# A fused attention and feed-forward layer on one core: shift rows issued ahead of the gap stores and key strips, and the early double steps closed up by two places

## What is computed

```python
q = (x @ wq).reshape(B, S, 16, 16); k = (x @ wk).reshape(B, S, 4, 16); v = (x @ wv).reshape(B, S, 4, 16)
q = q * cos + rotate_half(q) * sin;  k = k * cos + rotate_half(k) * sin
scores = einsum('bqkgd,bskd->bkgqs', q.reshape(B, S, 4, 4, 16), k) / sqrt(16)
out = einsum('bkgqs,bskd->bqkgd', softmax(scores), v).reshape(B, S, 256) @ wo
x = layernorm(x + out)
Wg, Wu, Wd = (gate_w - 128) * gate_scale[:, None], ...          # int32 weights, inner width 1024
x = layernorm(x + (silu(x @ Wg.T) * (x @ Wu.T)) @ Wd.T)
```

## Time and profile before

| | |
|---|---|
| median of 3 runs | 899.76 us |
| lowest, highest | 895.79, 901.49 us |
| profiled execution | 895.75 us, of which the span from first to last instruction is 893.9 us |
| PE busy | 873.9 us, 98% of the span |
| DVE, ACT, POOL busy | 740.8, 711.2, 272.4 us |
| mean granted TensorE clock | 0.995 |

### The profile page before, as it was taken

How to read it: one execution, slowest core, us unless ns; L and a number is a source line. 1 busy time by engine, 2 the same in 40 slices (tenths; PEclk the granted TensorE clock), 3 DMA queues, 4 the chain that set the end, 5 groups by cost and what they waited for, 6 DMA issues and landing times.

```text
span 893.9 us, 16212 instructions
## 1 busy us (share of the span) xinstructions
PE 873.9 (98%) x5658; PEld 457.1 (51%) x5658; DVE 740.8 (83%) x1653; ACT 711.2 (80%) x928; POOL 272.4 (30%) x236
## 2 busy tenths in 40 slices
PE   9999999999999999999999999999999999999996
PEld 3334334444444444434444444444436888888885
DVE  5679889999999999999999999999955455665545
ACT  2468889999999999999999999999985466555564
POOL 6564540045334010001001000210104665665555
PEclk9999999999999999999999999999999999999998
DMA  8973543423342122122223313121112010110001
GB/s 302 259 199 105 145 117 90 95 76 86 105 114 58 45 78 71 52 70 67 52 59 82 74 45 78 45 70 31 35 55 57 25 48 24 48 48 25 25 24 48
DMA packets 53458, 69.98 MB, mean 78 GB/s; under 512 B 17344, under 2 KB 26560, under 8 KB 53376
## 3 DMA queue, kind: packets, MB, share of 16 engines
q1 hardware_dynamic: 50280, 65.53, 26.8%
q0 software_dynamic: 864, 3.15, 1.2%
q10 hardware_dynamic: 2232, 0.25, 0.2%
HBM read 46.74 MB, written 16.25 MB: 70 GB/s over the span
## 4 chain that ended last, share of the span: by engine, by line
PE 86%; DVE 5%; SPq 3%; ACT 2%; DMA 2%; issue 2%; POOL 0%; POOLq 0%; DVEq 0%; ACTq 0%
PE pv_bank L1434 26%; PE ring_bank L1344 24%; PE pair_bank L1493 13%; PE pair_bank L1562 12%; PE pv_bank L1588 3%; PE ring_bank L1588 3%; PE ring_bank L1444 2%; DVE block_max L907 2%; PE pair_bank L1382 1%; ACT probs L1246 1%; DMA ident<-identity 1%; SPq L351 1%; PE ring_bank L1459 1%; DVE above L903 1%; SPq L491 1%
## 5 line engine op out<-in xcount | busy, mean ns | idle before, releaser
L1246 ACT ACTIVATE probs<-pair_bank 128x1024 f32<-128x1024 f32 x512 | 495.9, 1023 | 46.6 <-PE pair_bank L1493 46.5
L907 DVE TENSOR_REDUCE block_max<-ring_bank 128x1 f32<-128x384 f32 x854 | 486.3, 609 | 16.5 <-PE ring_bank L1344 6.4
L1344 PE MATMUL ring_bank<-k_max,q_sb 48*128 48x512 f32 x1122 | 309.0, 441 | 3.0 <-DMA k_max<-k_parts 1.4
L1344 PEld LDWEIGHTS ring_bank<-k_max,q_sb 48*128 48x128 f32 x1122 | 148.4, 184 | 268.8 <-DVE block_max L907 118.2
L1434 PE MATMUL pv_bank<-probs,v_all 128*17 128x512 f32 x2048 | 270.5, 600 | 0.6 <-ACT probs L1246 0.5
L1493 PE MATMUL pair_bank<-q_sb,k_sb 50*128 50x512 f32 x1024 | 219.8, 426 | 5.5 <-DMA q_sb<-shift 2.2
L1099 DVE SCALAR_TENSOR_TENSOR hid<-pair_bank,up_s,silu 128x512 f32<-128x512 f32 x63 | 47.1, 748 | 84.6 <-ACT silu L1304 84.6
L1493 PEld LDWEIGHTS pair_bank<-q_sb,k_sb 50*128 50x128 f32 x1024 | 97.8, 185 | 32.5 <-ACT probs L1246 6.4
L727 POOL TENSOR_TENSOR attn<-attn,inv_rows 128x1024 f32<-128x1024 f32 x7 | 16.7, 2384 | 301.4 <-DMA inv_rows<-inv_d 301.4
L812 POOL TENSOR_TENSOR hid_l<-hid,hid_h 128x512 fp32r<-128x512 f32 x63 | 81.7, 1297 | 86.1 <-ACT hid_h L1283 85.4
L1191 ACT ACTIVATE above<-ring_bank 128x512 f32<-128x512 f32 x138 | 81.9, 597 | 15.9 <-PE ring_bank L1344 10.1
(11 more groups left out here) (149 smaller groups left out, 863.0 us busy)
## 6 DMA issues: line engine op xcount, KB each, us to landing
k_max<-k_parts SPq DMA_DIRECT2D x96, 96.0 KB, 3.1
q_sb<-q_parts SPq DMA_DIRECT2D x64, 128.0 KB, 2.9
k_sb<-k_parts SPq DMA_DIRECT2D x96, 64.0 KB, 2.4
attn<-xT SPq DMA_DIRECT2D x8, 512.0 KB, 7.2
q_parts<-high SPq DMA_DIRECT2D x16, 256.0 KB, 3.5
q_parts<-low SPq DMA_DIRECT2D x16, 256.0 KB, 3.9
q_sb<-q_parts SPq DMA_DIRECT2D x64, 64.0 KB, 3.0
attn<-pv_sb SPq DMA_DIRECT2D x128, 32.0 KB
```

The lines of the kernel that those rows point to most:

```text
L907: dve.reduce_max(block_max[half % 2][:, col:col + 1], bank[:, 0:width], axis=AX.X).then_inc(ring_used, 1)
L1246: act.activation(probs[t % 2][:, 2 * pr:2 * pr + 2, :], pair_bank[pr][:], ACT.Exp, scale=D ** -0.5).then_inc(probs_ready, 1)
L1344: pe.matmul(bank[:, 0:last - first], q_sb[k][rows, i, qt * P:(qt + 1) * P], k_max[k // QH][rows, kind * CH + first:kind * CH + last], star ...
```

## The change

SP's order in pair 0: `load_shift` now stands ahead of `store_gap(k)` and `swap_strips(k+1)`; `swap_strips(1)` keeps its place. `load_scales` goes from half 1 of pair 0 to half 1 of pair 1. The twelve double steps are spread over 22 places in place of 24: they stand on 24, 25, 27, 29, 31, 33, 35, 36, 38, 40, 42, 44, that is (4,0), (4,1), (4,3), (4,5), (5,1), (5,3), (5,5), (6,0), (6,2), (6,4), (7,0), (7,2).

```diff
+LAST_STEP = 46
@@
         for i in range(2 * LEAD):
-            early[divmod(FIRST_STEP + i // 2 * (BLOCKS * HOOKS - FIRST_STEP) // LEAD, HOOKS)].extend(step(i))
+            early[divmod(FIRST_STEP + i // 2 * (LAST_STEP - FIRST_STEP) // LEAD, HOOKS)].extend(step(i))
@@
                         store_pv(p - 1 if k == 0 else p, (k - 1) % HALVES)
-                    if first and k > 0:
-                        store_gap(k)
-                        if k < B - 1:
-                            swap_strips(k + 1)
@@
                         load_shift(p + 1, 0)
                     if first and k == 0:
                         prologue_over()
-                        swap_strips(1)
+                    if first and k > 0:
+                        store_gap(k)
                     if first and k < B - 1:
+                        swap_strips(k + 1)
                         bring_half(k + 1)
                         store_k(k + 1)
-                    if first and k == 1:
+                    if p == 1 and k == 1:
                         load_scales()
```

## The result

The changed kernel took 901.32 us in the median of 20 runs (897.56 to 905.27), against 899.60 us for 20 runs of the kernel before. The ratio is **1.0026, 95% interval 1.0014 to 1.0038**: 2.3 us slower, where 2.2 us faster were forecast. Nine microseconds would be 1%, so this is a small loss, but it has the wrong sign.

The account below looks back on a forecast made before the run. PE was taken as the bound, busy 873.9 of 893.9 us, so queue edits pay only where PE stands still. The terms -2.36 (SP's order) and +0.2 (start) gave -2.2, from 899.76 to 897.6 us, range 892 to 901.5.

Parts of the forecast that it names:

- The two stalls: PE idle 1.90 us ahead of half 2 and 2.16 us ahead of half 3 in pair 0, together costing 4.27 us.
- the order is not what delays PE: Rival: ACT's writes or DMA queues delay the shift rows; stalls stay or shrink little, 899.3 us; chance 0.15.
- with the longer `load_q`: Variant for half 3 in pair 0: load_q takes 2.91 us, 0.6 us of stall stays, gain 1.3 us.
- Part 1: Shift rows ahead in SP's queue, pair 0: two old stalls go, one new comes; gain 2.36 us.
- The second stall goes too: Ahead of half 3: PE may start at 123.76 and wants it at 124.18, 0.4 us to spare.
- From the strips' end to the low key store 4.86: SP's queue, pair 0: strips' landing and POOL's work take 4.86 us and move with the strips.
- A new stall of 1.9 us: Ahead of half 4: SP's backlog lets PE start at 144.96, where it wants 143.05.
- I take nothing for it: Clock at the loop's start, half 0: a smoother start might return 1.7 to 3.4 us; counted as zero.
- Part 3: Closer double steps in the prologue: first scores 0.4 to 1.7 us later, DVE gives back up to 1.5; 0.2 us slower.
- the first shift rows come late: Rival, prologue: place (6,2) slips by d, first scores by d - 0.3; outweighs 2.36 from d = 2.7; 902.3 us; chance 0.10.
- A cover of 0.3 us: Prologue: the last first shift row lands at 63.7, PE's first scores start at 64.15; slack put at 0.3 us.
- Part 2: load_scales moved: frees 1.98 us of SP in pair 0's half 1; costs nothing in pair 1, at most 1.98 us.

Follow-up runs that it names:

- experiment 1: Only the closer double steps (22 places), SP's order as in the kernel before: 900.6 us, ratio 1.0008 to the kernel before.
- experiment 2: Changed kernel with the double steps on the old 24 places, so only SP's order and the scales move: 899.99 us, ratio 1.0000 to the kernel before.
- experiment 4: Changed kernel with SP's first shift rows issued ahead of block 5's second query store: 897.72 us, ratio 0.9984 to the kernel before.
- experiment 12: The kernel of experiment 2 run again, unchanged, for a second trace: 897.02 us.
- experiment 3: The kernel of experiment 2 with the gap stores moved behind the strips: 894.79 us, ratio 0.9946 to the kernel before.
- experiment 5: The changed kernel itself again, on a second chip: 901.2 us, ratio 1.0004 to the kernel before.
- experiment 11: The kernel before run again, unchanged, for a second trace: 900.47 us, an execution near its median.
- experiment 10: Experiment 3 (double steps on 24 places) with the first shift rows ahead of block 5's second query store: 894.39 us, ratio 0.9956 to the kernel before.
- experiments 13 to 15: Experiment 3's SP order, one chip, ratios to kernel before: 22 places with early first shift rows 0.9938; 24 places with them 0.9953; 22 places without 0.9952.
- experiment 6: Experiment 3 with the closer double steps on 22 places: 897.26 us, ratio 0.9967 to the kernel before.
- experiment 8: Experiment 3 with load_scales back in half 1 of pair 0: 894.74 us, ratio 0.9944 to the kernel before.

## Why the prediction was wrong

The forecast was 2.2 us faster: 2.4 from SP's order, less 0.2 for the start. Measured were 2.3 us slower, and 0.4 for the same kernel on a second chip. The experiments give nothing for SP's order. For the start the traces give about 1.6 us of loss, and experiment 1 gives 0.7, with an interval from 0.5 gained to 2.0 lost.

**What held.** The two stalls are SP's order, not ACT's writes and not the DMA queues, so the rival "the order is not what delays PE" falls. The stall ahead of half 2 goes in all five traces of the changed order (the changed kernel twice, experiments 2, 4 and 12), and a new one comes ahead of half 4 for the reason given; experiment 3 cuts it to 0.67 us by SP's order alone. In the profiled execution halves 1 to 4 gained 1.42 us of the 2.36, close to the 1.3 us that the prediction gives "with the longer `load_q`". That is luck: `load_q` was not the cause, and the four other traces of this order gained next to nothing there.

**First failed step: the 2.36 us of Part 1.** Forecast were 77.4 us for halves 1 to 4. Experiment 4 has 79.6 without any half clock, and experiments 2, 5 and 12 have 79.5 to 79.8 once the excess of half 4 over 18.87 us is taken out, against 79.75 in the profile of before. The 2.2 us that are missing are three terms:

- "The second stall goes too": 0.62 to 0.65 us of it stay in all five traces. "From the strips' end to the low key store 4.86" was 6.24 in the profile and 5.7 to 6.3 in the others, since POOL got its strips late: in the profile one of their four DMAs took 3.3 us to land and the others 2.0 to 2.1.
- "A new stall of 1.9 us" is 2.46 to 2.50 us in four traces, and 1.18 only in the profiled one. In the four the strips of the second pass took 3.2 to 3.5 us to issue, in the profile 2.45.
- A half between stalls was taken at its steady 18.87 us. Half 2 lost another 0.70 to 1.07, in all five traces together with a DVE shift instruction that ended just after POOL's. This term was put at nothing without a word; moving the strips back also moved POOL's work under DVE's.

**The clock: a term left out, but not the cause of this loss.** "I take nothing for it" was said of the start alone, and stalls were priced at their length. They are the start of half-clock stretches too: 10.2, 6.8 and 3.4 us behind the new stall in experiments 2, 5 and 12, and 10.2 us behind the second stall of the kernel before in experiment 11. It is tempting to say that the change turned a gain into a clock loss. The runs don't bear it out: the mean granted clock of the changed kernel is 0.9911 and, on the second chip, 0.9918, that of the kernel before there 0.9885. SP's order alone gains nothing at equal clock either (experiment 2). What the clock does show is why an order that leaves no stall over 0.7 us gains 4.9 us, more than the 3.4 us of its halves 1 to 4, and why one forced stall costs 7.5. Within a kernel a run's span falls as its mean clock rises: the correlation is -0.8 to -0.95 in each kernel up to experiment 10, and -0.1 to -0.9 on the chip of experiments 13 to 15, with 6 to 11 runs each. On the chip of experiments 1 to 4 the kernel before has 894.3 to 895.2 us of span in runs at 0.993 and 898.6 to 900.1 at 0.986. The prediction saw the profile at 0.995 lie 4.0 us under the median and shifted it by 4.0 without asking for their cause.

**Second failed step: "I take 0.2 us slower" of Part 3.** The start lost 2.71 us, not 0.4 to 1.7: 1.66 by PE itself, and 1.05 by shift rows that came late. Bank waits come to about 2.57 us (at (4,1), (5,3), (6,0) and (6,4)) against 1.7 in the kernel before; the rest fits the projections that now stand alone between steps (the key and value projection of a block took 2.02 us in two parts and 1.87 in one). Half 0 gave back 22.29 - 21.20 = 1.09 us, within the 1.5 of Part 3, and the profile lost 1.6 in all; experiment 1 measured 0.7, experiment 6 against 3 1.9. The 1.6 lie outside Part 3's own ends, of which the upper, 1.2, left out that the whole 1.7 could be lost. That is the rival "the first shift rows come late". Its deciding point was d = 2.7, and d was 2.84. Its price came from the rows of the prologue; what it lacked was a chance above 0.10. Its 902.3 us lie near the 901.32 measured, but that is in part luck: it has the 2.36 us of Part 1 in it, which did not come, and a second half-clock stretch at the start, which the profile does not have. "A cover of 0.3 us" in the earlier trace rows was the warning: any delay beyond it goes to the end in full.

**Part 2** is tested only on the repaired order: there the scales cost nothing in pair 0 (experiment 8). In pair 1 they may not be free, as Part 2 had it: 11 of the 13 traces with the scales moved have a wait of 0.10 to 0.49 us ahead of the first scores of half 6, the four without the move have none. That is small, and no experiment was made on it.

**The sum.** Parts alone: 1.0008 and 1.0000. Together 1.0026 and 1.0004, which agree with each other and with the sum only at their edges. The changed kernel is 0.4 to 2.3 us slower: a start that got 1.6 us longer, and a gain that was laid out from one trace and isn't there in the others.

**What stays open.** Why a stall of about 2.5 us is followed by 0, 3, 7 or 10 us at half clock in kernels that are alike there; no run here separates the cases. (The Trainium skill, "TensorE: Matmul & The Clock Gate", section "What's actually happening", says that the gate's watch runs free and doesn't start with the kernel, so that one kernel meets it in another phase each time. The unequal stretches behind equal stalls agree with that, and show no more of it.) And why one strip DMA lands late: in all five traces of the changed order it coincides with a transfer of 0.02 MB by an instruction queue, which in both traces of before falls on `load_scales` or `load_q` instead (the longer `load_q` of Part 1). In the four traces with a new stall of 2.5 us a second such transfer falls into the slow strips of the second pass, 1.3 to 1.8 us after their start; in the profiled execution it comes 1.5 us after their end. These are coincidences in time; no experiment moved one. In the changed kernel, DMA activity from 109 to 110 us, its instruction queue (packets, MB, share) and the strip DMA under way (KB, us to landing):

```profile
q8 instruction: 1, 0.02, 7.1%
...
k_by_sin<-k_turn SPq DMA_DIRECT2D x1, 64.0 KB, 3.3
```

## What to carry to other kernels

Before pricing a stall by its length, look whether the profiled execution is a usual one: if its clock and time are the best of its runs, take another trace near the median, and look for half-clock stretches behind the same stall. Before calling the clock the cause, compare the mean granted clocks of the two kernels over all runs, and their times at the same clock. Where stalls of one cause come in a row, an edit that leaves one long one may gain nothing; here what paid was to leave none over 0.7 us. A reordering shifts the other engines' work too: look what it now runs beside. In a queue that waits for another engine's answer, put the request first (the strips) and fill the wait with what nobody needs (the gap stores); and before closing work up ahead of a chain with 0.3 us of cover, move that chain's own issue forward.

## What the runs showed of the hardware

TensorE's granted clock fell from 2.4 to 1.2 GHz within 2 us of the end of stalls of 1.95 to 2.52 us in a PE that was busy before (experiments 1, 2, 5, 11, 12), for 3.4 to 10.2 us. It stayed up behind stalls of 2.46 us (experiment 4), 2.51 (ahead of half 2 in experiment 11), and 1.90 and 2.16 us. A stall 3.85 us longer than before cost 7.5 us with the half clock behind it, and about 4 in the runs without. A DVE instruction that writes `shift_rows` took 0.68 to 0.78 us instead of 0.17 when it met POOL's `gap_l`, and ended 0.03 to 0.04 us after it, in all five traces of the changed order. The key and value projection of a block took 2.02 us in two parts with a double step between them and 1.87 in one. On SP each of its small DMAs took 0.57 to 0.68 us to issue; the useless ones of 512 bytes, at 0.68, were no quicker than the shift rows' 2 KB at 0.57.
